# A mixture-of-experts kernel on one core: the transposes of gathered rows in F32R instead of fp32

## What is computed

```python
def _L0_attn_ref(x, Wqkv, bqkv, Wout, bout):          # 16 heads of 16, band of 64 to either side
    ...
def _moe_forward(x, router_w, router_b, w1, b1, w2, b2, top_k=2):
    logits = jnp.einsum('bsd,de->bse', x, router_w) + router_b
    top_vals, top_idx = jax.lax.top_k(logits, top_k)
    ...
    h = jax.nn.relu(jnp.einsum('td,edh->eth', xf, w1) + b1[:, None, :])
    y = jnp.einsum('eth,ehd->etd', h, w2) + b2[:, None, :]
    out = jnp.einsum('etd,te->td', y, gf)
...
xn = _layernorm(x, axis=-1)
x = x + _L0_attn_ref(xn, ...) + _L0_ffn_ref(xn, ...)
```

## Time and profile before

| what | us |
|---|---|
| median of 3 runs | 971.83 (971.32 to 981.16) |
| the profiled execution | 980.77 |
| its span, first to last instruction | 978.7 |
| PE busy in the span | 920.3 (94%) |
| DVE busy | 816.5 (83%) |
| ACT busy | 739.8 (76%) |
| POOL busy | 497.9 (51%) |
| mean granted TensorE clock | 0.984 of full |

### The profile page before, as it was taken

The page is one execution under the profiler, slowest core; times in us unless marked ns, Lnnn a source line. Parts: engine busy times, 40 slices in busy tenths (PEclk is TensorE's granted clock), DMA queues, the critical chain, the costliest instruction groups (busy, mean ns, idle before and its releaser), DMA issues. The chain is left out here.

```text
span 978.7 us, 27549 instructions
## 1 busy us (share of the span) xinstructions
PE 920.3 (94%) x7684; PEld 893.4 (91%) x7684; DVE 816.5 (83%) x2170; ACT 739.8 (76%) x1983; POOL 497.9 (51%) x699
## 2 busy tenths in 40 slices
PE   4899799899999999999939999999999999999996
PEld 4788788889999999999829999999999999999996
DVE  5876799988888888888738888888888888888885
ACT  4445799889999999999816777677777666777773
POOL 5210014145555555555534666666666666666663
PEclk9999799999999999999969999999999999999999
DMA  4889324434444444444224212222212222221210
GB/s 152 311 291 308 124 74 119 127 104 149 136 133 135 136 135 136 135 138 130 80 88 112 42 32 41 44 36 36 37 29 42 45 48 43 34 43 34 36 21 1
DMA packets 69868, 95.34 MB, mean 97 GB/s; under 512 B 15550, under 2 KB 48961, under 8 KB 69697
## 3 DMA queue, kind: packets, MB, share of 16 engines
q1 hardware_dynamic: 52800, 77.97, 25.9%
q0 software_dynamic: 17024, 16.88, 10.8%
HBM read 62.91 MB, written 35.53 MB: 101 GB/s over the span
## 5 line engine op out<-in xcount | busy, mean ns | idle before, releaser
L1007 ACT ACTIVATE weights_qkv<-weights_qkv,low 128x256 f32<-128x256 f32 (+1 forms) x512 | 240.2, 480 | 1.3 <-DVE low L818 1.3
L1416 ACT ACTIVATE hid<-ps_experts,b_s 128x256 f32<-128x256 f32 x312 | 130.8, 473 | 133.7 <-PE ps_experts L1482 133.1
L1303 POOL DMA_INDIRECT out<-y,target x78 | 153.6, 1969 | 123.5 <-DVE y L1382 107.2
L829 DVE TENSOR_TENSOR pt<-ps_attend,pt 128x512 fp32r<-128x512 f32 (+1 forms) x256 | 158.4, 620 | 39.2 <-ACT pt L1020 24.9
L1097 PE MATMUL ps_attend<-pt,v_m 128*80 128x256 f32 (+7 forms) x1536 | 187.1, 271 | 2.3 <-DVE inv_t L842 1.6
L1498 PE MATMUL ps_experts<-w_hi,h_hi 128*128 128x256 f32 x624 | 178.6, 286 | 0.8 <-DVE h_lo L1350 0.7
L1482 PE MATMUL ps_experts<-xgt_hi,w_hi 128*128 128x256 f32 x624 | 175.8, 282 | 1.7 <-DVE xgt_lo L1341 1.7
L1498 PE MATMUL ps_experts<-w_hi,h_lo 128*128 128x256 f32 x624 | 175.3, 281 | 0.0
L1498 PE MATMUL ps_experts<-w_lo,h_hi 128*128 128x256 f32 x624 | 175.3, 281 | 0.0
L1482 PE MATMUL ps_experts<-xgt_hi,w_lo 128*128 128x256 f32 x624 | 175.0, 280 | 0.0
L1482 PE MATMUL ps_experts<-xgt_lo,w_hi 128*128 128x256 f32 x624 | 174.9, 280 | 0.0
(11 more groups left out here) (164 smaller groups left out, 2009.2 us busy)
## 6 DMA issues: line engine op xcount, KB each, us to landing
weights_qkv<-in_w SPq DMA_DIRECT2D x15, 1024.0 KB
qk_hi<-weights_qkv SPq DMA_DIRECT2D x16, 512.0 KB, 4.9
qk_lo<-weights_qkv SPq DMA_DIRECT2D x16, 512.0 KB, 5.9
q_st<-qk_hi SPq DMA_DIRECT2D x128, 64.0 KB
k_st<-qk_hi SPq DMA_DIRECT2D x128, 64.0 KB
weights_qkv<-in_x SPq DMA_DIRECT2D x8, 512.0 KB, 4.3
xn_rows<-weights_qkv SPq DMA_DIRECT2D x8, 512.0 KB, 5.1
k_st<-qk_lo SPq DMA_DIRECT2D x64, 64.0 KB
```

Source lines behind the costliest of these rows:

```text
L829: v.tensor_tensor(lo[:, f:l], ps[:, bank_t[h], 0:l - f], hi[:, f:l].bitcast(F32), ALU.subtract).then_inc(s_plo, 1)
L1007: ins = act.activation(wt[:, ring, at_tile(i)], wt[:, ring, at_tile(i)], ACT.Exp, bias=low[:, ring, i:i + 1], scale=-1.0, accum_out=total[ ...
L1303: pool.indirect_dma_start(out_tokens, bass.IndirectOffsetOnAxis(ap=target[:, h:h + 1], axis=0), y[:, h], None, bounds_check=T - 1, oob_is_ ...
L1416: ins = act.activation(hid[:, n % 2, j], ps[:, bank_h[n], j * ROWS:(j + 1) * ROWS], ACT.Relu, bias=b1[:, ds(e * FC + 2 * n + j, 1)])
```

## The change

Inside `experts`, the three row buffers `xg` are declared as F32R instead of fp32, and a second identity `ident_r`, F32R, is made by a DVE copy of `g.ident` ahead of the memsets. The four transposes of a step take the F32R rows and the F32R identity and write PSUM through an F32R view. The gather and the memsets write the same words through an fp32 view; ACT and DVE read PSUM as fp32 as before. PE waits once, before the first transposes, for the identity copy. Everything else is the same.

```diff
-        xg = sb("xg", [P, RING, 2, D])
+        xg = sb("xg", [P, RING, 2, D], F32R)
+        ident_r = sb("ident_r", [P, P], F32R)
...
+        s_ident_r = sem("s_ident_r", "v")
...
-                            xg[:, ring, h], None, g.xn_dram,
+                            xg[:, ring, h].bitcast(F32), None, g.xn_dram,
...
+                v.tensor_copy(ident_r[:], g.ident[:]).then_inc(s_ident_r, 1)
                 for ring in range(RING):
-                    v.memset(xg[:, ring], 0.0).then_inc(s_xz, 1)
+                    v.memset(xg[:, ring].bitcast(F32), 0.0).then_inc(s_xz, 1)
...
-                            ins = pe.transpose(ps[:, bank_t, (c * 2 + h) * P:(c * 2 + h + 1) * P],
-                                               xg[:, ring, h, c * P:(c + 1) * P], g.ident[:])
+                            ins = pe.transpose(ps[:, bank_t, (c * 2 + h) * P:(c * 2 + h + 1) * P].bitcast(F32R),
+                                               xg[:, ring, h, c * P:(c + 1) * P], ident_r[:])
                     ins.then_inc(s_tr, 1)
 
+                pe.wait_ge(s_ident_r, 1 + START)
                 transpose_rows(0, 0)
```

## The result

The changed kernel took 962.67 us (961.58 to 963.56, 4 runs) against 972.09 us for the kernel before on the same chip: a ratio of 0.9875 with a 95% interval of 0.9833 to 0.9916. A second set of runs on another chip gave 963.44 against 971.72 us, 0.9908 (0.9892 to 0.9925).

A forecast was written before the change was run, and what follows sets the result against it. The prediction took PE's sequence of loads and matmuls to bound the experts' stage. Transposes -4.1, identity copy +0.25 and first group -0.2 gave -4.05 us, so 971.83 became 967.8 us, range 964.0 to 975.0.

The forecast's parts named there:

- What bounds the kernel: Experts' stage: PE's own sequence of loads and matmuls bounds it, busy 431.52 of 431.52 us, no other engine full.
- Term (a): Experts' steps: four transposes in F32R shorten each of 38 steps by 108 ns, 4.1 us in all.
- spacing of 70 ns: L1468: F32R transposes would start 70 ns apart instead of 109, after the short F32R streams at L1070 and L1071.
- The way out of the group: Last transpose to layer 2's second matmul: 118 + 118 ns, the first 118 being that layer's ordinary load.
- The sum: Whole kernel: -4.1 + 0.25 - 0.2 = -4.05 us, subtracted from the median 971.83, gives 967.8 us; chance 0.50.
- Term (b): Ahead of the row-tile memsets: the DVE identity copy adds 0.25 us, all on the path to the first transpose.
- Term (c): First four transposes, at half clock after PE idleness: F32R would save 0.2 us, paying for the identity copy.
- What is late next: Feeders of PE in the steps: xgt_lo has 1.07 us of slack before layer 1, so the gain passes through.
- A: L1468 transposes: F32R needs the same two cycles a column, spacing stays 109 ns; 972.1 us, chance 0.26.
- B: L1468: F32R transposes load like other F32R operands, 118 ns a pair, 36 ns more a step; 973.5 us, chance 0.18.
- C: L1468: F32R leaves the transpose form, each call two passes, 236 ns, 312 records; 991 us, chance 0.04.
- faster by over 1%: Whole kernel: would need more than the 4.8 us the transposes can give at any row's price; chance 0.04.

The follow-up runs named there:

- the second trace of before: The kernel before, unchanged, run again for another trace: 971.38 us, with 20 of 38 steps in the 113.3 ns matmul spacing.

## Why the prediction was wrong

**What bounds the kernel.** Right: PE bounds the steps before and after (from 540 to 930 us it is busy all the time in both).

**Term (a), the transposes.** The mechanism was right, the size was not. The F32R identity streams shorter and the short load stays (142 ns). The forecast was 108 ns a step; measured between fast steps of both kernels it is 82 ns, 3.1 us in 38 steps instead of 4.1. What failed is the spacing of 70 ns taken from L1070 and L1071: the first two are below it (58 and 63 ns), then it is 87, and 86 with eight in a row. The way out of the group was misread too. The sum puts 109 and 118 ns behind the last fp32 transpose, where the earlier trace rows have 28 and 201 ns, nearly the same together. It forecast 118 and 118 behind the last F32R one, and there are 87 and 194, 45 ns more.

**Term (b), the copy of the identity.** Right in size, 0.19 us on the path against 0.25. The copy took 0.23 us:

```profile
499.65 0.23 DVE L1355 CAST ident_r<-ident 128x128 fp32r<-128x128 f32 x1 [4.06 <-PEq L612]
...
507.97 0.72 PE L1471 MATMUL ps_experts<-ident_r,xg 128*128 128x128 f32 x4 [13.18 <-DMA xg<-xn_rows,index]
```

The first transposes start only 0.03 us later than in the earlier trace rows (507.97 against 507.94), but the attention part happened to end earlier in this run: its last DVE instruction ended 0.15 us sooner. What compares is PE's idle time ahead of them, 13.18 us against 12.99 in the earlier trace rows, 0.19 us more. The kernel with the copy and fp32 transposes has 13.17, the second trace of before 12.99. It is not the copy alone: the memsets are put off by 0.22 us, the index copy behind them on POOL takes 1.05 us instead of 1.23, and from the landing of the gather to the first transpose it is 0.25 us instead of 0.09. The last is where PE has its added wait, which the forecast put at nothing; no run separates the three. In the ten runs with the copy and fp32 transposes, 0.02% of the time cannot be seen (ratio 0.9995).

**Term (c), the first group at the half clock.** It fell from 1.10 to 0.74 us by the chain, 0.36 us, against 0.2 forecast, at a granted clock of 0.50 in both.

**What is late next.** Right that PE waits for no engine in the steps, but with little left. DVE's idle time for the hidden layer fell from 49.6 to 27.6 us (five more casts lie in the later window), and `xgt_lo` now comes just in time:

```profile
L1350 DVE CAST h_hi<-hid 128x512 fp32r<-128x512 f32 x154 | 72.3, 469 | 27.6 <-ACT hid L1419 20.1 <-issue 6.3
...
612.73 0.68 DVE L1343 TENSOR_TENSOR xgt_lo<-ps_experts,xgt_hi 128x512 fp32r<-128x512 f32 x1
613.70 0.19 PEld L1486 LDWEIGHTS ps_experts<-xgt_hi,w_hi 128*128 128x128 f32 x1
```

From the end of `xgt_lo` (613.41) to the first load of layer 1 it is 0.30 us in two steps of three, where it was 0.96 before. 0.22 us of it pass even when PE waits, as the run without transposes shows, so 0.08 us are left. The forecast read 1.07 us of slack up to the matmul, and counted neither its load nor this delay. A next saving of 0.1 us a step on PE alone would meet DVE.

**The sum: the step that failed.** It treated the 118 ns between matmuls as a fixed price of the F32R load and subtracted only what the transposes give. That spacing is not fixed: the same 96 matmuls of a step start 117.8 or 113.3 ns apart. 7 us of the result, more than two thirds, are in it: 18 more fast steps than the second trace of before has, times 0.398, are 7.2 us. With 3.1 for the transposes that is 10.3, and 463.1 - 452.6 = 10.5 us are measured from the first transpose on. The two profiled executions differ by less, 971.38 - 962.66 = 8.7 us, since the first transposes came at 506.2 us in one and 508.0 in the other; the medians differ by 9.4 and 8.3 us. "The terms are differences and its steps are bound by PE cycles, so I subtract from the median" was the error in one sentence: the profiled execution and the median of before differed by 9 us, and this difference was left unexplained. 7.7 of the 9.4 us between the first and the second trace of before are the same effect, the rest is the attention part. The table and the trace of before held two hints, that difference and the last layer 2 at 113.3 ns.

**The rivals.** A (no change of spacing) and B (118 ns from a long load) fall by the line L1471: 250 ns streams, 142 ns loads. C falls by the 156 records. The Trainium skill's "TensorEngine Tiling (Array Packing)", section Restrictions, names FP32 and FP32R together as the inputs of the transpose mode. The trace agrees as far as the load goes, 141 and 142 ns; read as "alike in time" it does not hold, with 109 ns between fp32 and 86 between F32R transposes. The chance for faster by over 1% was put at 0.04, with the argument that the transposes cannot give more. They did not; the rest came from instructions that the argument had left out. That 0.04 also had no case of its own among the rivals, where all that lies outside them has 0.02. Of the signs named, the shorter streams (250 for about 225), the group (0.46 us for 0.43), the loads and the later start came about as said; the step's period did not, 11.27 us instead of 11.65, and this is where the second effect shows.

**What stays open.** Why there are two rhythms, and what chooses. The type of the four transposes decides how often the fast one is chosen (0 or 20 of 38 for fp32, 37 or 38 for F32R), but one, two or three F32R streams of four give 0, 29 and 13. The patterns repeat exactly, every 1, 3, 4 or 6 steps (apart from the first few), and at the last layer 2, with no transposes between, the rhythm changed sides in 13 of 13 traces. That suggests that what PE did just before layer 2, and the instant at which layer 2 meets it, decide; this is argued, not shown. F32R transposes in the attention part were not run.

## What to carry to other kernels

Where PE is full, transposes through an F32R view cost less than fp32 ones (86 against 109 ns each in a row). Before pricing a change in such a stage, read the spacing of the unchanged matmuls in more than one trace: if the profiled execution and the median of the runs differ by 1%, find out in which rows, since a small edit can move the kernel from one course to the other and give more, or take more, than its own instructions. Compare per step, between steps of the same rhythm, to price the edit itself. And compare a delay by the idle time ahead of an instruction, not by its start in two executions, since whole parts ahead of it end at other instants (2.6 us here). When a stage gets shorter, read again how close its feeders are: here `xgt_lo` went from 0.96 to 0.30 us ahead, 0.22 of which cannot be used.

## What was not expected of the hardware

- The same stream of F32R loads and matmuls (128 columns loaded, 256 streamed) runs at 113.3 or 117.8 ns a pair at the same granted clock of 1.00. Behind transposes it keeps one for 96 matmuls, across the border between layer 2 and layer 1, in every step of these traces.
- F32R transposes of 128x128 start 58, 63 and then 86 to 88 ns apart, fp32 ones 109.
- With no transposes between them, the last layer 2 started in the other rhythm than the layer 1 before it, in 13 of 13 traces.
- Leaving out 152 transposes of 156 saved 1 us against the changed kernel, because PE began to wait for DVE, with a loop of 11.20 to 11.25 us a step against the 11.27 of the changed kernel. The slow rhythm returned in most layers 1, behind these waits.
